# Last attention of a small vision tower: the mask multiply moves to GpSimd, one more group is scaled by ScalarE, and GpSimd's folding is cut in three

## The chip, the cores and the metric

The kernel runs on one core of a Trainium2 chip. The metric is the device time of one execution in microseconds; the time of a version is the median of its runs. Engines are called PE (TensorE), DVE (VectorE), ACT (ScalarE), POOL (GpSimd) and SP (SyncE) as in the profile.

## The reference

The program is a whole tower: 16 images of 36 tokens of 192 features go through a token embedding and four layers, each an attention-like block and a feed-forward block with residual additions. Only the attention of the last layer (L3) is touched:

```
q, k, v = split((layernorm(h) @ W_qkv + b_qkv), 12 heads of 16)
w = einsum('bhqd,bhkd->bhqk', q, k) * 16 ** -0.5       # 16 x 12 x 36 x 36
kth = top_k(w, int(0.4 * 36) = 14)[0][..., -1:]
w = where(w >= kth, w, min_val)
attn = softmax(w)
h = h + einsum('bhqk,bhkd->bqhd', attn, v).reshape(16, 36, 192) @ W_proj + b_proj
```

The feed-forward block behind it is a mixture of 16 experts with a layer norm (gain `ln_w`) ahead of each expert's second matrix. The gain can be multiplied into that matrix beforehand; this "folding" is done during the attention.

## The kernel before

The stage `layer3_attention` starts with a layer norm and the projections, then `head_attention` works on the scores. They lie as 108 rows (3 heads x 36 queries) by 64 columns of 36 keys: `sc` is `[108, 64, 36]`, a view of `padded`, whose rows are 64 apart. The 64 are cut into four groups (`BATCHES = 4`) of `CH = 16`, so one group is 108 x 576 numbers. There is no scheduler: each engine runs its own list in the order written, and semaphores join the lists.

For group g the work goes around the engines:

- PE makes the scores; ACT (`scores`, L677) copies them out of PSUM.
- DVE, `lower(g)`: top 8 of each row (L748, 16 instructions), replace them (L751, 16), top 8 of the rest (L754, 16), the maximum into `mx` (L757 or L759), and the mask `kept = (sc >= 14th)` (L760). For a group that is not `early` it then subtracts the maximum (L768).
- ACT, `exponentials(g)`: for an early group 16 instructions of 36 columns with the maximum as bias (L684), else one of 576 columns (L687). They raise `exps`.
- DVE, `normalize(g)`: multiply by `kept` (L775), sum (L776), reciprocal (L778 or L780). For an early group this raises `inverted` and ACT scales, 16 instructions of 36 columns (`scale`, L694, raising `act_probs`); else DVE scales (L781, raising `probs`).
- PE, `turn(g)` (L637): transposes the probabilities; it waits for `act_probs` or `probs`. ACT, `take_turned(g)`: first `scale(g)`, then two copies out of PSUM (L702). PE, `apply(g)` (L654): times v. ACT, `add_bias(g)` (L707).

Before, groups 0 and 1 are early (`early = BATCHES - 2`). DVE's list is lower(0), lower(1), normalize(0), lower(2), normalize(1), lower(3), normalize(2), normalize(3). ACT's list behind the scores is exponentials(0), (1), take_turned(0), exponentials(2), take_turned(1), a small copy (`keep_shifts`, L845), add_bias(0), exponentials(3), take_turned(2), add_bias(1), take_turned(3), add_bias(2), (3). PE's is `multiply` of experts 0 to 8 (L830), turn(0), `multiply` of experts 9 to 15, turn(1), apply(0), turn(2), apply(1), turn(3), apply(2), apply(3), and then the output projection (L3348).

`SecondWeights.fold` on POOL multiplies the second matrix of experts 1 to 15 by its gain, one instruction of 128 x 576 each (L840), in one loop; each waits for PE's `multiply` of the same expert. POOL does nothing else while the scores are worked on but one memset (L604).

The same `head_attention` serves the attention of layer L1 with `sparse=False` and without `also`; there `early` is 0.

Of the kernel before, what the change touches and what calls it, by code (L numbers as in the profile page):

```python
# [17 lines left out]
ALU = mybir.AluOpType  # L18
# [85 lines left out]
class Tower:  # L104
# [42 lines left out]
    def sem(self, name):  # L147

        s = self.nc.alloc_semaphore(name)
        self.of_layer.append(s)  # L150
        return s
# [409 lines left out]
def head_attention(T, ctx, block, name, ready, qk, wide, v, vb, att, sparse, also=None, space=None):  # L561
# [6 lines left out]
    BATCHES = 4  # L568
    PER = IMAGES // BATCHES
    CH = 4 * PER  # L570
# [11 lines left out]
    mx = sb("mx", [ROWS, NG])  # L582
    total = sb("total", [ROWS, NG])
    pt = sb("pt", [128, IMAGES, 2, H3, SEQ]) if space is None else space[1]
    early = BATCHES - 2 if sparse else 0
    inverted, act_probs = sem("inverted"), sem("act_probs")
    scored, sc_in, lowered, exps, probs, turned, cleared, pt_in, pv, att_in, step = map(
        sem, ("scored", "sc_in", "lowered", "exps", "probs", "turned", "cleared", "pt_in", "pv", "att_in",
              "dve_step"))
# [11 lines left out]
    @block.gpsimd  # L601
    def _(pool):
        ready(pool, True)
        pool.memset(padded[:, :, SEQ:TALL], 0.0).then_inc(cleared, 1)  # L604

    @block.tensor
    def _(pe):
# [129 lines left out]
    def _(dve):  # L737
        link = chained(dve, step)

        def lower(g):  # L740
            dve.wait_ge(sc_in, 2 * (g + 1))
            n = range(CH * g, CH * g + CH)
            part = sc[:, CH * g:CH * g + CH, :]
            top = mx[:, CH * g:CH * g + CH]
            if sparse:

                for i in n:
                    ins = dve.max(top8[:, i, :], sc[:, i, :])  # L748
                link(ins)
                for i in n:  # L750
                    ins = dve.match_replace(kept[:, i, :], top8[:, i, :], sc[:, i, :], -3.0e38)  # L751
                link(ins)
                for i in n:
                    ins = dve.max(next8[:, i, :], kept[:, i, :])  # L754
                link(ins)
                if g < early:
                    link(dve.tensor_scalar(top, top8[:, CH * g:CH * g + CH, 0], -1.0, None, ALU.mult))  # L757
                else:
                    link(dve.tensor_copy(top, top8[:, CH * g:CH * g + CH, 0]))  # L759
                link(dve.tensor_tensor(kept[:, CH * g:CH * g + CH, :], part,  # L760
                                       next8[:, CH * g:CH * g + CH, KEEP - 9:KEEP - 8].broadcast_to([ROWS, CH, SEQ]),
                                       ALU.is_ge))
            else:
                link(dve.tensor_reduce(top, part, AX.X, ALU.max))
            if g < early:
                dve.sem_inc(lowered, 1)
            else:
                dve.tensor_tensor(part, part, spread(top, 2, SEQ), ALU.subtract).then_inc(lowered, 1)  # L768

        def normalize(g):  # L770
            dve.wait_ge(exps, g + 1)
            part = sc[:, CH * g:CH * g + CH, :]
            tot = total[:, CH * g:CH * g + CH]
            if sparse:
                link(dve.tensor_tensor(part, part, kept[:, CH * g:CH * g + CH, :], ALU.mult))  # L775
            link(dve.tensor_reduce(tot, part, AX.X, ALU.add))  # L776
            if g < early:
# [4 lines left out]

        lower(0)
        lower(1)
        normalize(0)
        lower(2)
        normalize(1)
        lower(3)
        normalize(2)
        normalize(3)  # L790
# [6 lines left out]
class SecondWeights:  # L797
# [33 lines left out]
                               start=(e == 0 and f == 0), stop=(e == self.E - 1 and f == self.C - 1))  # L831
            mm.then_inc(self.summed, 1)

    def fold(self, pool):

        for e in range(1, self.E):
            w = cols(self.w[:, e, 0:self.C * DIM], self.C)
            gain = self.w[:, e, self.C * DIM:self.C * DIM + self.C]
            pool.wait_ge(self.summed, e + 1)
            pool.tensor_tensor(w, w, spread(gain, 2, DIM), ALU.mult).then_inc(self.folded, 1)  # L840
        pool.wait_ge(self.folded, self.E - 1)

    def keep_shifts(self, act, bank):
        act.wait_ge(self.summed, self.E)
# [2473 lines left out]
def layer3_attention(T):  # L3318

    nc, p = T.nc, T.p  # L3320
    with ExitStack() as ctx:
# [10 lines left out]
        att_in = head_attention(T, ctx, block, "a3_att", ready, qk, wide, v, p["avb"], att, True, second)  # L3332
        proj = cols(p["aproj"], 2)

        @block.gpsimd
        def _(pool):
            second.fold(pool)

        def at(s):
            return slice(HALF * s, HALF * s + HALF)  # L3340

# [244 lines left out]
```

## Time and profile before

| | |
|---|---|
| median of 3 runs | 841.12 us (840.67 to 842.9) |
| profiled execution | 844.89 us |
| its span in the trace | 843.0 us |
| PE busy | 749.0 us (89%) |
| DVE busy | 378.4 us (45%) |
| ACT busy | 306.2 us (36%) |
| POOL busy | 273.4 us (32%) |
| scores made to output projection of this stage | about 661 to 714 us of the span |

The profiled execution is 3.8 us above the median of the runs; a change inside it is read from its own rows and carried to the median as a difference. Times in a timeline count from the span's start. Busy shares over the whole span say little on this stage: it has 53 us of 843, and in it DVE is busy nearly throughout and PE has gaps.

### The profile page before, as it was taken

The numbers are of one execution on the slowest core, as the hardware profiler recorded it, in microseconds if no ns is written. First come the engines' busy times: TensorE is split into PE (matmuls) and PEld (weight loads), VectorE is DVE, ScalarE is ACT, GpSimd is POOL, SyncE is SP. The second block draws the span as 40 slices with busy tenths as digits, with TensorE's granted clock in tenths as the row PEclk, the third lists the DMA queues.
The fourth block names the chain that finished last, engine by engine and source line by source line (L and its number), as shares of the span: only waits on it lengthen the run. The fifth ranks groups of instructions, "written<-read, shape, count | busy, mean of one in ns | idle before, by whom it ended". The sixth has DMA issues, their size and how long they took to land. (4 is left out here: it accounts for less than half of the span.)

```text
span 843.0 us, 15814 instructions
## 1 busy us (share of the span) xinstructions
PE 749.0 (89%) x5369; PEld 558.3 (66%) x5369; DVE 378.4 (45%) x1111; ACT 306.2 (36%) x723; POOL 273.4 (32%) x316
## 2 busy tenths in 40 slices
PE   8996999798999988999977899997898967989885
PEld 5774888465585657999744788873455656666663
DVE  1354222234263257788595122221153695645543
ACT  2530222223464047666331122222234453524440
POOL 0004455100002116676023544443301161045770
PEclk9997999998989999999999999999999889879995
DMA  9815889400000052220041879626554030811224
GB/s 355 337 32 166 275 276 289 144 1 1 1 3 1 0 215 70 70 75 14 1 148 31 296 240 391 194 55 207 195 126 160 29 99 3 315 41 53 69 73 98
DMA packets 39254, 108.50 MB, mean 129 GB/s; under 512 B 5616, under 2 KB 12736, under 8 KB 38672
## 3 DMA queue, kind: packets, MB, share of 16 engines
q1 hardware_dynamic: 31584, 88.35, 30.7%
q0 software_dynamic: 7600, 19.25, 8.6%
q8 instruction: 40, 0.66, 0.3%
q14 instruction: 30, 0.25, 0.1%
HBM read 95.88 MB, written 11.70 MB: 128 GB/s over the span
## 5 line engine op out<-in xcount | busy, mean ns | idle before, releaser
L1431 POOL TENSOR_TENSOR ssm_w_low<-ssm_wbc,ssm_w_high 128x512 fp32r<-128x512 f32 x24 | 31.1, 1300 | 38.5 <-ACT ssm_w_high L1386 38.5
L157 ACT ACT_TABLE_LOAD x19 | 24.4, 1283 | 49.1 <-PEq L162 48.9
L2056 POOL TENSOR_TENSOR L_s_up<-L_s_hid,L_s_up 116x288 f32<-116x288 f32 (+1 forms) x10 | 8.3, 828 | 103.6 <-ACT L_s_up L2050 103.6
L1836 DVE TENSOR_TENSOR L_act_many<-L_hid,bank 116x384 f32<-116x384 f32 x28 | 15.5, 554 | 57.0 <-ACT L_hid L1716 44.8
L1346 PE MATMUL bank<-ssm_x_high,ssm_w_high 128*128 128x288 f32 x96 | 33.8, 352 | 3.8 <-DVE bank L1474 2.3
L1441 POOL TENSOR_TENSOR ssm_grown<-ssm_less,xn 128x576 f32<-128x576 f32 x23 | 32.9, 1430 | 8.0 <-ACT ssm_less L1414 5.3
L1691 POOL DMA_INDIRECT y_rows_L<-L_many_y,L_many_rows_out x21 | 20.7, 988 | 44.4 <-ACT L_many_y L1734 37.1
L1716 ACT ACTIVATE L_hid<-bank 116x384 f32<-116x384 f32 x28 | 13.7, 490 | 56.8 <-PE bank L1767 38.4
L1480 DVE TENSOR_TENSOR_SCAN ssm_state<-ssm_decay,bank 128x576 f32<-128x576 f32 x24 | 32.5, 1354 | 0.8
L2025 PE MATMUL bank<-xn,par_L1f 128*116 128x288 f32 (+1 forms) x128 | 31.0, 455 | 0.1
L1666 POOL DMA_INDIRECT L_many_xr<-x_rows_L,L_many_rows_in x27 | 26.8, 994 | 11.9 <-issue 10.6
L2981 DVE TENSOR_TENSOR L_act<-L_hid,bank 128x384 f32<-128x384 f32 x18 | 10.0, 554 | 45.1 <-ACT L_hid L2950 32.4
L1346 PE MATMUL bank<-ssm_x_low,ssm_w_high 128*128 128x288 f32 x96 | 28.8, 300 | 0.0
L1346 PE MATMUL bank<-ssm_x_high,ssm_w_low 128*128 128x288 f32 x96 | 28.7, 299 | 0.0
L1346 PE MATMUL bank<-ssm_x_mixed,ssm_w_high 128*128 128x288 f32 x96 | 28.6, 298 | 0.0
L1346 PE MATMUL bank<-ssm_x_top,ssm_w_low 128*128 128x288 f32 x96 | 28.5, 297 | 0.0
L1356 PE MATMUL bank<-ssm_out,ssm_sum_w 128*128 128x288 f32 x96 | 27.3, 406 | 0.0
L2950 ACT ACTIVATE L_hid<-bank 128x384 f32<-128x384 f32 x18 | 8.8, 489 | 50.5 <-PE bank L2920 50.5
L2868 POOL DMA_INDIRECT y_rows_L<-L_yb,L_rows_out x18 | 17.8, 989 | 24.9 <-ACT L_yb L2956 21.6
L297 PE MATMUL bank<-h,par_const 128*128 128x288 f32 x64 | 19.1, 446 | 7.4 <-PEq L162 7.4
L3077 PE MATMUL bank<-L_w,L_xtb 128*128 x68 | 24.8, 486 | 0.0
L1762 PE MATMUL bank<-L_many_xt,L_w 128*116 128x192 f32 x128 | 24.6, 335 | 0.0
(550 smaller groups left out, 1938.4 us busy)
## 6 DMA issues: line engine op xcount, KB each, us to landing
L_w<-in_L2w SPq DMA_DIRECT2D x14, 696.0 KB, 7.1
L_more<-in_L2w SPq DMA_DIRECT2D x10, 696.0 KB
L_w<-in_L0w SPq DMA_DIRECT2D x12, 576.0 KB
ssm_wbc<-in_wBC SPq DMA_DIRECT2D x24, 256.0 KB
L_w<-in_L3w SPq DMA_DIRECT2D x5, 1152.0 KB
L_w<-in_L2w SPq DMA_DIRECT2D x14, 384.0 KB
L_more<-in_L0w SPq DMA_DIRECT2D x9, 576.0 KB
second<-in_L3w SPq DMA_DIRECT2D x16, 291.0 KB
```

The source lines that it names most:

```text
L157: self.nc.scalar.activation(self.unread[:, at:at + 1], self.p["ones"][:, 0:1], func)
L297: mm = pe.matmul(T.bank[s][:, 0:HALF], mean[:, c, :], self.x[:, c, HALF * s:HALF * s + HALF], start=(c == 0), stop=(c == 1))
L1346: mm = pe.matmul(T.bank[2 * a + s][:, 0:HALF], w[t % NW][:, at:at + 128], x[:, HALF * s:HALF * s + HALF], start=(n == 0), stop=(n == len(t ...
L1356: mm = pe.matmul(T.bank[2 * SUM_AT + s][:, 0:HALF], sum_w[t % NB][:, :], out[t % NB][:, HALF * s:HALF * s + HALF], start=t in (0, REST_TILES),
L1431: pool.tensor_tensor(w_low[t % NW][:, :], wbc[t % NW][:, :], w_high[t % NW][:, :], ALU.subtract).then_inc(low, 1)
L1441: pool.tensor_tensor(grown[t % NB][:, :], less[t % NB][:, :], xs[:, of(t), :], ALU.mult).then_inc(grown_made, 1)
L1480: dve.tensor_tensor_scan(st[:, :], d[:, :], drive, 0.0, ALU.mult, ALU.add).then_inc(scanned, 1)
L1666: pool.indirect_dma_start(self.xr[j][:, :], None, self.X.x_rows[:, :], bass.IndirectOffsetOnAxis(ap=self.rows_in[h][:, u:u + 1], axis=0))\
L1691: pool.indirect_dma_start(X.y_rows[:, :], bass.IndirectOffsetOnAxis(ap=self.rows_out[h][:, u:u + 1], axis=0), self.y[U * h + u][:, :], Non ...
L1762: pe.matmul(bank[0:N, MANY * f:MANY * f + MANY], w1[:, at:at + N], self.xt[h][:, 0, rows], start=(f == 0), stop=False)
L2025: mm = pe.matmul(self.T.bank[bank + u % self.RING][0:self.N, 0:HALF], self.w1[lanes, c, at:at + self.N], self.T.xn[lanes, c, HALF * s:HALF ...
L3077: mm = pe.matmul(self.up_bank[u % 2][:, 0:I], self.X.xt[u % 4][:, c, :], self.w1[:, bass.ds(e * (2 * I) + (I * c - 2 * I), I)], start=(c = ...
```

## The change

Three edits, all in the sparse case of `head_attention`:

1. `early` goes from 2 to 3: group 2 gets its exponentials in 16 ACT instructions with a bias, no subtraction on DVE, and is scaled by ACT in 16 instructions and not by DVE.
2. For the three early groups POOL multiplies `sc` by `kept` (new L609) once ACT has raised `exps`, and raises `masked`; DVE's `normalize` waits for that and only sums and inverts. Group 3 is multiplied by DVE as before.
3. The folding goes into POOL's list in parts: experts 1 to 4 behind the multiply of group 0, 5 to 8 behind that of group 1, 9 to 15 behind that of group 2. On DVE, normalize(0) and (1) move behind the first 16 instructions of lower(2) and lower(3).

```diff
--- before.py
+++ after.py
@@ -582,8 +582,8 @@
     mx = sb("mx", [ROWS, NG])
     total = sb("total", [ROWS, NG])
     pt = sb("pt", [128, IMAGES, 2, H3, SEQ]) if space is None else space[1]
-    early = BATCHES - 2 if sparse else 0
-    inverted, act_probs = sem("inverted"), sem("act_probs")
+    early = BATCHES - 1 if sparse else 0
+    inverted, act_probs, masked = map(sem, ("inverted", "act_probs", "masked"))
     scored, sc_in, lowered, exps, probs, turned, cleared, pt_in, pv, att_in, step = map(
         sem, ("scored", "sc_in", "lowered", "exps", "probs", "turned", "cleared", "pt_in", "pv", "att_in",
               "dve_step"))
@@ -602,6 +602,13 @@
     def _(pool):
         ready(pool, True)
         pool.memset(padded[:, :, SEQ:TALL], 0.0).then_inc(cleared, 1)
+        if also:
+            for g in range(early):
+                at = slice(CH * g, CH * g + CH)
+                pool.wait_ge(exps, g + 1)
+                pool.tensor_tensor(sc[:, at, :], sc[:, at, :], kept[:, at, :], ALU.mult).then_inc(masked, 1)
+                also.fold(pool, 4 * g + 1, min(4 * g + 5, also.E) if g < early - 1 else also.E)
+            pool.wait_ge(also.folded, also.E - 1)
 
     @block.tensor
     def _(pe):
@@ -747,6 +754,8 @@
                 for i in n:
                     ins = dve.max(top8[:, i, :], sc[:, i, :])
                 link(ins)
+                if g >= 2:
+                    normalize(g - 2)
                 for i in n:
                     ins = dve.match_replace(kept[:, i, :], top8[:, i, :], sc[:, i, :], -3.0e38)
                 link(ins)
@@ -768,10 +777,13 @@
                 dve.tensor_tensor(part, part, spread(top, 2, SEQ), ALU.subtract).then_inc(lowered, 1)
 
         def normalize(g):
-            dve.wait_ge(exps, g + 1)
             part = sc[:, CH * g:CH * g + CH, :]
             tot = total[:, CH * g:CH * g + CH]
-            if sparse:
+            if g < early:
+                dve.wait_ge(masked, g + 1)
+            else:
+                dve.wait_ge(exps, g + 1)
+            if sparse and g >= early:
                 link(dve.tensor_tensor(part, part, kept[:, CH * g:CH * g + CH, :], ALU.mult))
             link(dve.tensor_reduce(tot, part, AX.X, ALU.add))
             if g < early:
@@ -782,9 +794,11 @@
 
         lower(0)
         lower(1)
-        normalize(0)
+        if not sparse:
+            normalize(0)
         lower(2)
-        normalize(1)
+        if not sparse:
+            normalize(1)
         lower(3)
         normalize(2)
         normalize(3)
@@ -831,14 +845,13 @@
                                start=(e == 0 and f == 0), stop=(e == self.E - 1 and f == self.C - 1))
             mm.then_inc(self.summed, 1)
 
-    def fold(self, pool):
-
-        for e in range(1, self.E):
+    def fold(self, pool, first, end):
+
+        for e in range(first, end):
             w = cols(self.w[:, e, 0:self.C * DIM], self.C)
             gain = self.w[:, e, self.C * DIM:self.C * DIM + self.C]
             pool.wait_ge(self.summed, e + 1)
             pool.tensor_tensor(w, w, spread(gain, 2, DIM), ALU.mult).then_inc(self.folded, 1)
-        pool.wait_ge(self.folded, self.E - 1)
 
     def keep_shifts(self, act, bank):
         act.wait_ge(self.summed, self.E)
@@ -3332,10 +3345,6 @@
         att_in = head_attention(T, ctx, block, "a3_att", ready, qk, wide, v, p["avb"], att, True, second)
         proj = cols(p["aproj"], 2)
 
-        @block.gpsimd
-        def _(pool):
-            second.fold(pool)
-
         def at(s):
             return slice(HALF * s, HALF * s + HALF)
 
```

DVE's list, from the last two instructions of lower(1), twelve rows. `a_att_sc` are the scores, `a_att_kept` the mask, `a_att_top`, `a_att_next` the top values, `a_att_mx` the maxima, `a_att_total` the sums. Before:

```order
L757 TENSOR_SCALAR a_att_mx<-a_att_top 108x16
L760 TENSOR_TENSOR a_att_kept<-a_att_sc,a_att_next 108x576
L775 TENSOR_TENSOR a_att_sc<-a_att_sc,a_att_kept 108x16x36
L776 TENSOR_REDUCE a_att_total<-a_att_sc 108x16
L778 RECIPROCAL a_att_total<-a_att_total 108x16
L748 MAX a_att_top<-a_att_sc 108x8 x16
L751 MATCH_REPLACE a_att_kept<-a_att_top,a_att_sc 108x36 x16
L754 MAX a_att_next<-a_att_kept 108x8 x16
L759 COPY a_att_mx<-a_att_top 108x16
L760 TENSOR_TENSOR a_att_kept<-a_att_sc,a_att_next 108x576
L768 TENSOR_TENSOR a_att_sc<-a_att_sc,a_att_mx 108x16x36
L775 TENSOR_TENSOR a_att_sc<-a_att_sc,a_att_kept 108x16x36
```

And in the changed kernel, from the same place:

```order
L766 TENSOR_SCALAR a_att_mx<-a_att_top 108x16
L769 TENSOR_TENSOR a_att_kept<-a_att_sc,a_att_next 108x576
L755 MAX a_att_top<-a_att_sc 108x8 x16
L788 TENSOR_REDUCE a_att_total<-a_att_sc 108x16
L790 RECIPROCAL a_att_total<-a_att_total 108x16
L760 MATCH_REPLACE a_att_kept<-a_att_top,a_att_sc 108x36 x16
L763 MAX a_att_next<-a_att_kept 108x8 x16
L766 TENSOR_SCALAR a_att_mx<-a_att_top 108x16
L769 TENSOR_TENSOR a_att_kept<-a_att_sc,a_att_next 108x576
L755 MAX a_att_top<-a_att_sc 108x8 x16
L788 TENSOR_REDUCE a_att_total<-a_att_sc 108x16
L790 RECIPROCAL a_att_total<-a_att_total 108x16
```

The multiply by the mask (L775) has left the list; the sum and the reciprocal stand between the first and the second kind of instruction of the next group; group 2 has a TENSOR_SCALAR for its maximum (L766) and no subtraction.

ACT's list from the scaling of group 0 to the copies of group 2. Before:

```order
L694 ACTIVATE a_att_sc<-a_att_sc,a_att_total 108x36 x16
L702 COPY a_att_pt<-bank 128x432 x2
L687 ACTIVATE a_att_sc<-a_att_sc 108x16x36
L694 ACTIVATE a_att_sc<-a_att_sc,a_att_total 108x36 x16
L702 COPY a_att_pt<-bank 128x432 x2
L845 ACTIVATE sw_shift<-bank 16x192
L707 ACTIVATE a_att<-bank,par_L3a 96x144 x2
L687 ACTIVATE a_att_sc<-a_att_sc 108x16x36
L702 COPY a_att_pt<-bank 128x432 x2
```

And in the changed kernel (L701 is the scaling, L691 and L694 the two kinds of exponential, L709 the copies):

```order
L701 ACTIVATE a_att_sc<-a_att_sc,a_att_total 108x36 x16
L709 COPY a_att_pt<-bank 128x432 x2
L691 ACTIVATE a_att_sc<-a_att_sc,a_att_mx 108x36 x16
L701 ACTIVATE a_att_sc<-a_att_sc,a_att_total 108x36 x16
L709 COPY a_att_pt<-bank 128x432 x2
L858 ACTIVATE sw_shift<-bank 16x192
L714 ACTIVATE a_att<-bank,par_L3a 96x144 x2
L694 ACTIVATE a_att_sc<-a_att_sc 108x16x36
L701 ACTIVATE a_att_sc<-a_att_sc,a_att_total 108x36 x16
```

Group 2's one exponential is now 16, and 16 instructions of scaling stand ahead of its copies.

POOL's list behind its memset was one row before, fifteen times L840. In the changed kernel it is (L609 the multiply by the mask, L854 the folding):

```order
L609 TENSOR_TENSOR a_att_sc<-a_att_sc,a_att_kept 108x16x36
L854 TENSOR_TENSOR second<-second 128x576 x4
L609 TENSOR_TENSOR a_att_sc<-a_att_sc,a_att_kept 108x16x36
L854 TENSOR_TENSOR second<-second 128x576 x4
L609 TENSOR_TENSOR a_att_sc<-a_att_sc,a_att_kept 108x16x36
L854 TENSOR_TENSOR second<-second 128x576 x7
```

The folding of experts 1 to 4, 5 to 8 and 9 to 15 now stands behind one multiply each.

## Rows read from the trace of the kernel before

**Rows 1.** Waits between 662 and 716 us: engine, line, released by: total, times, longest.
```profile
PE bank L637 <- ACT a_att_sc L694: 6.4, 1, 6.4
PE bank L637 <- DVE a_att_sc L781: 3.8, 1, 3.8
```

**Rows 2.** Timeline of PE: start us, us, instruction, count, idle before it.
```profile
686.50 3.20 PE L637 MATMUL bank<-par_const,a_att_sc 108*64 108x108 f32 x32 [6.43 <-ACT a_att_sc L694]
689.43 7.57 PE L830 MATMUL bank<-second,sw_cols 128*48 128x192 f32 x42
696.84 1.70 PE L637 MATMUL bank<-par_const,a_att_sc 108*64 108x108 f32 x32
...
703.00 2.12 PE L637 MATMUL bank<-par_const,a_att_sc 108*64 108x108 f32 x32 [3.80 <-DVE a_att_sc L781]
...
706.16 2.45 PE L637 MATMUL bank<-par_const,a_att_sc 108*64 108x108 f32 x32
...
709.82 4.15 PE L3348 MATMUL bank<-a_att,par_L3a 96*128 96x288 f32 x16
```

**Rows 3.** Timeline of ACT.
```profile
679.45 3.55 ACT L684 ACTIVATE a_att_sc<-a_att_sc,a_att_mx 108x36 f32<-108x36 f32 x16 [4.91 <-DVEq L766]
682.91 3.54 ACT L694 ACTIVATE a_att_sc<-a_att_sc,a_att_total 108x36 f32<-108x36 f32 x16
...
689.74 0.52 ACT L702 COPY a_att_pt<-bank 128x432 f32<-128x432 f32 x1 [0.92 <-PE bank L637]
690.15 0.69 ACT L687 ACTIVATE a_att_sc<-a_att_sc 108x576 f32<-108x576 f32 x1
691.58 3.55 ACT L694 ACTIVATE a_att_sc<-a_att_sc,a_att_total 108x36 f32<-108x36 f32 x16 [0.74 <-DVE a_att_total L778]
...
699.47 0.64 ACT L707 ACTIVATE a_att<-bank,par_L3a 96x144 f32<-96x144 f32 x2
700.44 0.68 ACT L687 ACTIVATE a_att_sc<-a_att_sc 108x576 f32<-108x576 f32 x1 [0.33 <-DVE a_att_sc L768]
```

**Rows 4.** Timeline of DVE.
```profile
671.04 1.66 DVE L748 MAX8 a_att_top<-a_att_sc 108x8 f32<-108x36 f32 x16
...
677.18 0.49 DVE L757 TENSOR_SCALAR a_att_mx<-a_att_top 108x16 f32<-108x16 f32 x1
677.71 1.66 DVE L760 TENSOR_TENSOR a_att_kept<-a_att_sc,a_att_next 108x576 f32<-108x576 f32 x1
679.51 1.47 DVE L775 TENSOR_TENSOR a_att_sc<-a_att_sc,a_att_kept 108x576 f32<-108x576 f32 x1
681.01 0.75 DVE L776 TENSOR_REDUCE a_att_total<-a_att_sc 108x16 f32<-108x576 f32 x1
681.80 0.25 DVE L778 RECIPROCAL a_att_total<-a_att_total 108x16 f32<-108x16 f32 x1
...
689.72 0.75 DVE L775 TENSOR_TENSOR a_att_sc<-a_att_sc,a_att_kept 108x576 f32<-108x576 f32 x1
...
704.72 0.76 DVE L781 TENSOR_TENSOR a_att_sc<-a_att_sc,a_att_total 108x576 f32<-108x576 f32 x1
```

**Rows 5.** Timeline of POOL in narrow stretches; the last row a whole run of folds.
```profile
677.60 1.14 POOL L840 TENSOR_TENSOR second<-second 128x576 f32<-128x576 f32 x1
678.71 1.65 POOL L840 TENSOR_TENSOR second<-second 128x576 f32<-128x576 f32 x1
...
691.22 7.78 POOL L840 TENSOR_TENSOR second<-second 128x576 f32<-128x576 f32 x7 [8.13 <-PE bank L830]
```

**Rows 6.** An earlier line of POOL: count, then ns min/median/max, first and last start.
```profile
L1441 POOL TENSOR_TENSOR ssm_grown<-ssm_less,xn x23: 1415/1428/1439, 323.4 to 399.6; 128x576 f32<-128x576 f32 x23
```

**Rows 7.** Windows: us, busy (count) of PE, PEld, DVE, ACT, POOL, clock, DMA share, GB/s.
```profile
686.40:690.00 3.60, 3.50 (x34) 3.34 (x35) 3.50 (x20) 0.83 (x3) 0.00 (x0) 0.50 0.00 0
...
697.00:700.00 3.00, 2.19 (x81) 1.94 (x77) 2.90 (x9) 1.89 (x5) 2.00 (x2) 1.00 0.00 0
...
704.20:707.60 3.40, 3.40 (x76) 3.06 (x73) 1.46 (x4) 1.53 (x4) 0.00 (x0) 0.50 0.02 5
```

## Prediction

> **What bounds the kernel now.** Only the stretch from the scores to the output projection of the last attention is edited, so I read the waits of that stretch first, then the timelines of its engines. The waits show where PE, which carries the stage to its end, stands still: 6.4 us for ACT's scaling of group 0 and 3.8 us for DVE's scaling of group 2 [rows 1]. On PE's timeline these are the gaps ahead of 686.50 and 703.00; turn(1) at 696.84 has no gap ahead of it, since the multiply of experts 9 to 15 runs until then; and from 703.00 on PE runs without a gap to the projection at 709.82 [rows 2]. So the end is set by when turn(2) starts, and what it waits for.
>
> Two chains lead there. DVE's: it works from 671.04 to 705.48 [rows 4], and its scaling of group 2 is what released turn(2) at 703.00 [rows 1, 2]. ACT's: group 1's exponentials 679.45 to 683.00, scaling of group 0 until 686.45, turn(0), its second copy until 690.26, exponential of group 2 (0.69), scaling of group 1, copies, a bias that ends at 700.11, exponential of group 3 at 700.44 [rows 3]. That last row waited only 0.33 us for DVE: ACT's chain is just behind DVE's already. The reader is to see that the two are nearly level, so that work cannot be moved from DVE to ACT for nothing.
>
> **What DVE loses.** Three multiplies by the mask, one subtraction and one scaling, all of 108 x 576 with two inputs: 0.75 us each where nothing disturbs them, 1.47 us for the one at 679.51 [rows 4]. That is 5 x 0.75 plus 0.7, about 4.4 us, and if DVE alone set turn(2) this would be the gain. Moving normalize(0) behind the first sixteen instructions of lower(2) costs nothing: ACT can't scale group 0 before its exponentials of group 1 end at 683.00, and these start when lower(1) ends.
>
> **What ACT gets.** Group 2's exponentials as sixteen take 3.55 us instead of 0.69, and its scaling is 3.55 more [rows 3]. I walk the chain with before's times. After the second copy of turn(0), ACT starts the sixteen exponentials at 690.15; they end at 693.70, the scaling of group 1 at 697.25. Turn(0) began 0.05 us after its scaling, so turn(1) begins at 697.30 instead of 696.84 (PE's multiply hid the rest). Before, ACT was free for group 3's exponential 3.27 us after turn(1) began (696.84 to 700.11); now at 700.60. It takes 0.68, then comes the new scaling, 3.55: 704.83. Turn(2) starts at 704.88 instead of 703.00: **+1.88 us**. Nothing hides it, for PE stands idle already.
>
> **What POOL gets.** Each multiply by the mask is bounded from below by a fold, 1.14 us, and from above by the undisturbed 1.44 of a multiply of 128 x 576 with two full inputs [rows 5, 6]; I take 1.43, as the kept mask too is a full input. None lies on the path: the one of group 0 starts at about 674.6 (3.55 us after the group's exponentials begin at about 671) and is wanted at 681. Then four folds at (7.78 - 1.15) / 6 = 1.11 us a step [rows 5] run until 680.4, ahead of the end of group 1's exponentials at 683.0; four more end by 689.4 and group 2's exponentials at 694. The last seven folds end near 705 instead of 699, where nothing waits for them before the block ends near 715.
>
> **What POOL does to DVE.** The fold that began at 677.60 held up the instructions at 677.18 (0.49) and, after the next small gap, at 677.71 (1.66 where 0.76 is usual), and the fold at 678.71 then took 1.65 instead of 1.14, the DVE instruction in between [rows 4, 5]: the two engines take turns, and a DVE instruction of two inputs that meets a fold loses up to about 1.1 us. The Trainium skill ("SBUF — State Buffer", section "Who interferes with whom") says that a Vector instruction with two SBUF inputs and a GpSimd one that reads SBUF exclude each other for the whole instruction, and that whichever was issued first holds the ports; this trace agrees (1.66 and 1.65 us where 0.76 and 1.14 are usual). The rule speaks against the change, since POOL gets 18 such instructions instead of 15 and spreads them over more of DVE's list: if the waits stayed as the rows of before have them, the sum below would be +1.2 us, and if each further meeting costs a wait, it is +2.2.
>
> I take two terms. First, lower(1): POOL's folds stand at 676.0, 677.1 and 678.2 now, so the maximum at 677.18 comes just behind the start of one and waits to 678.2, not 677.6; the end of lower(1), and all of ACT's chain with it, moves from 679.37 to 679.96, **+0.6**. Bounds: no meeting at all, 677.18 + 0.17 + 0.76 = 678.1, -1.2; the worst phase +0.7. Second, group 3: lower(2) took 6.14 us of its own kind from its start to the maximum (as 671.04 to 677.18 for the pass before [rows 4]); with the sum and the inverse (0.75 + 0.25) inside and two waits for folds lower(2) ends at about 690.1 and lower(3) finds its maximum at 697.3. Its last three instructions (copy, mask, subtraction) now fall into the seven folds, wait for one each, and end at about 701.2; before, POOL was done at 699.0 [rows 5] and they ended ahead of 700.44 [rows 3]. Sum and inverse of group 2 come behind them, 702.3, and ACT wants them at 701.3 + 0.6 = 701.9: **+0.4**, with 0 and +1.2 as bounds. DVE's 4.4 us are thus spent on waiting for POOL and on standing behind ACT. Group 3's probabilities, by the same rows about 706, are wanted at 708 or later.
>
> **PE's clock.** Turn(0) took 3.20 us at a granted clock of 0.50 (1.2 GHz), turn(1) 1.70 at 1.00 (2.4 GHz) [rows 2, 7]. Turn(2) to turn(3) took 2.12 and 2.45, because the clock fell to 0.50 from 704.2 to 707.6 after the idle time ahead of 703.00 [rows 2, 7]. With turn(2) at 704.88 + 0.6 + 0.4 = about 705.9, less work lies in that half-clock stretch: 1.7 us of it instead of 3.4, so half of 1.7 is regained, less a little for copies: **-0.7**, if the clock rises at the same place. If it doesn't, nothing is regained and about 0.8 more is lost.
>
> **Sum.** +1.88 + 0.6 + 0.4 - 0.7 = **+2.2 us**: the profiled execution from 844.9 to 847.1, and the median, which lies 3.8 below the profiled execution, from 841.12 to **843.3**.
>
> **Rivals.**
> - The clock stays low behind 707.6, since PE's pause ahead of turn(2) grows from 3.8 to above 5 us. Then the rest of turn(2), apply(1) and most of turn(3) run at half the clock until about 711: +1.5 on the forecast, +3.7, 844.8. For it speaks that turn(0) stayed at 0.50 after a pause of 6.4 us; against it, that 704.2 to 707.6 was followed by a rise with much the same work in it. This is the case slower by more than 0.3%; it decides if PE's start of turn(2) comes later than about 706. Chance 0.24.
> - DVE, not ACT, sets turn(2): every instruction of two inputs in lower(2) and lower(3) waits for a full fold, and the order to scale comes a microsecond and more later than I took: +3.2, 844.3, slower. Chance 0.14.
> - POOL misses DVE in lower(1) and half the half-clock loss goes too: 1.88 - 1.2 - 1.4 = -0.7, 840.4, faster but inside 0.3%. It needs the phase of POOL's folds to fall right. Chance 0.12. That more is gained needs ACT's sixteen to be quicker than its rows; 0.06 for all that.
> - The change does not do what it says: POOL reaches the multiply late, behind folds, and DVE waits for `masked`. The slack is 683.0 - 680.4 = 2.6 us at group 1 and about 4.9 at group 2; it decides only if a fold took 1.8 us or more. Chance 0.02, time 844 to 846.
>
> **How the numbers follow.** The forecast has 0.42; its own range is 841.5 to 843.9 (below, the first term at -1.2 in place of +0.6; above, the second at +1.0 in place of +0.4). A measurement of this kernel tells about 0.3%, 2.5 us, from no change, which is 843.6. Faster by that: 0.06. Slower: both slower rivals, 0.38, and a part of the forecast's upper edge beside a part of these two that stays below, 0.38 in all. Same: 0.56. The range for 8 in 10 is 841.2 to 845.2: from the lower end of the forecast's own to the clock rival with its spread.
>
> **What would show each step.** Right: ACT without a gap from turn(0)'s second copy to turn(1), two runs of 3.55 us; PE's wait ahead of turn(2) released by ACT's scaling and 5 to 6 us long; DVE's list shorter in instructions but ending after 704; DVE's mask instructions at 1.2 to 1.7 us in all four groups; POOL's multiplies at 1.4 us. Wrong: turn(2) released before 703, or released by DVE; mask instructions at 0.76 us; a multiply on POOL well over 2 us; the clock at 0.50 after 707.6.

## The result and the profile after

The changed kernel takes 847.65 us in the median (843.14 to 853.73, 9 runs), the kernel before beside it 841.71; the ratio is 1.0095, interval 1.0064 to 1.0126. It is slower: by 5.9 us as the medians stand, by 8 us (5.4 to 10.6) as the ratio does, where 2.2 were predicted. (Ratios here and below are of undisturbed executions and need not equal the quotient of two medians.) The profiled execution has a span of 849.7 us, 6.7 more than before's.

Executions differ by several us ahead of this stage, so I compare the **stretch** from DVE's first MAX8 of the stage to PE's first instruction of the output projection: 663.79 to 709.82 before [rows 2], **46.0 us**, and 665.50 to 719.23 after, **53.7 us**. The 7.7 us of difference are as large as the whole loss, so it arises here.

The waits of the changed kernel between 664 and 726 us (engine and line, released by: total, times, longest):

```profile
PE bank L644 <- ACT a_att_sc L701: 17.1, 2, 8.9
...
ACT a_att_sc L694 <- DVE a_att_sc L777: 3.5, 1, 3.5
```

PE's second pause grew from 3.8 to 8.9 us. It is released by ACT and no longer by DVE [rows 1], as predicted, though 5 to 6 us of it were expected; but ACT itself waits 3.5 us for DVE's subtraction of group 3, where it waited 0.33 [rows 3]. PE's timeline after, answering to [rows 2]:

```profile
689.93 3.20 PE L644 MATMUL bank<-par_const,a_att_sc 108*64 108x108 f32 x32 [8.15 <-ACT a_att_sc L701]
692.86 8.35 PE L844 MATMUL bank<-second,sw_cols 128*48 128x192 f32 x42
701.05 1.70 PE L644 MATMUL bank<-par_const,a_att_sc 108*64 108x108 f32 x32
...
712.34 3.20 PE L644 MATMUL bank<-par_const,a_att_sc 108*64 108x108 f32 x32 [8.94 <-ACT a_att_sc L701]
...
716.37 1.75 PE L644 MATMUL bank<-par_const,a_att_sc 108*64 108x108 f32 x32
...
719.23 4.15 PE L3357 MATMUL bank<-a_att,par_L3a 96*128 96x288 f32 x16
```

ACT's, answering to [rows 3]:

```profile
682.87 3.55 ACT L691 ACTIVATE a_att_sc<-a_att_sc,a_att_mx 108x36 f32<-108x36 f32 x16 [6.62 <-DVEq L775]
...
693.58 3.55 ACT L691 ACTIVATE a_att_sc<-a_att_sc,a_att_mx 108x36 f32<-108x36 f32 x16
697.03 3.54 ACT L701 ACTIVATE a_att_sc<-a_att_sc,a_att_total 108x36 f32<-108x36 f32 x16
...
703.68 0.64 ACT L714 ACTIVATE a_att<-bank,par_L3a 96x144 f32<-96x144 f32 x2
707.78 0.68 ACT L694 ACTIVATE a_att_sc<-a_att_sc 108x576 f32<-108x576 f32 x1 [3.46 <-DVE a_att_sc L777]
708.74 3.55 ACT L701 ACTIVATE a_att_sc<-a_att_sc,a_att_total 108x36 f32<-108x36 f32 x16 [0.27 <-DVE a_att_total L790]
```

And what DVE did meanwhile, answering to [rows 4]: of groups 1, 2 and 3 the instruction that writes 16 maxima, and the comparison behind it.

```profile
678.89 2.20 DVE L766 TENSOR_SCALAR a_att_mx<-a_att_top 108x16 f32<-108x16 f32 x1
681.13 1.65 DVE L769 TENSOR_TENSOR a_att_kept<-a_att_sc,a_att_next 108x576 f32<-108x576 f32 x1
...
689.96 1.29 DVE L766 TENSOR_SCALAR a_att_mx<-a_att_top 108x16 f32<-108x16 f32 x1
691.28 1.65 DVE L769 TENSOR_TENSOR a_att_kept<-a_att_sc,a_att_next 108x576 f32<-108x576 f32 x1
...
700.12 5.16 DVE L768 COPY a_att_mx<-a_att_top 108x16 f32<-108x16 f32 x1
705.31 1.65 DVE L769 TENSOR_TENSOR a_att_kept<-a_att_sc,a_att_next 108x576 f32<-108x576 f32 x1
706.99 0.76 DVE L777 TENSOR_TENSOR a_att_sc<-a_att_sc,a_att_mx 108x576 f32<-108x576 f32 x1
```

A copy of 16 elements a partition took 5.16 us. It takes 0.17 where nothing is in its way. POOL's timeline shows what was:

```profile
676.33 1.40 POOL L609 TENSOR_TENSOR a_att_sc<-a_att_sc,a_att_kept 108x576 f32<-108x576 f32 x1 [10.52 <-ACT a_att_sc L691]
677.71 4.45 POOL L854 TENSOR_TENSOR second<-second 128x576 f32<-128x576 f32 x4
686.50 1.40 POOL L609 TENSOR_TENSOR a_att_sc<-a_att_sc,a_att_kept 108x576 f32<-108x576 f32 x1 [4.34 <-ACT a_att_sc L691]
687.87 4.45 POOL L854 TENSOR_TENSOR second<-second 128x576 f32<-128x576 f32 x4
697.21 1.41 POOL L609 TENSOR_TENSOR a_att_sc<-a_att_sc,a_att_kept 108x576 f32<-108x576 f32 x1 [4.89 <-ACT a_att_sc L691]
698.57 7.78 POOL L854 TENSOR_TENSOR second<-second 128x576 f32<-128x576 f32 x7
```

The reader is to see the seven folds of the last row: 1.11 us apart, the COPY arrives at 700.12, in the second of them (699.68 to 700.8), and ends at 705.28, just as the last one begins at 705.20. Folds took 1.15 us each in that time, so POOL lost nothing; DVE waited through five of them, the one that ran and four that were let in ahead of it. In groups 1 and 2 the same instruction was passed over by one fold in a run of four, and the comparison behind it waited for the last fold.

Where the 7.7 us arise, as differences of the two timelines: first MAX8 to ACT's exponentials of group 1 (they start when lower(1) ends), 15.66 to 17.37, +1.7; turn(0) to turn(1), +0.8; turn(1) to the exponential of group 3, 3.60 to 6.73, +3.1; from there to turn(2), 2.56 to 4.56, +2.0; turn(2) to the projection, 6.82 to 6.89, +0.1.

The +0.8 is not ACT's. Its scaling of group 1 ended at 700.57, but PE's multiply ran until turn(1) at 701.05: it took 8.35 us, 7.57 before [rows 2], at a lower granted clock. The window of that multiply, columns as in [rows 7], before and after:

```profile
689.50:696.80 7.30, 7.30 (x45) 5.41 (x42) 7.16 (x62) 4.65 (x18) 5.58 (x6) 0.93 0.01 3
692.90:701.00 8.10, 8.10 (x45) 5.83 (x42) 7.82 (x68) 7.41 (x33) 3.79 (x4) 0.83 0.01 3
```

### The profile page after: what moved, and what is told of

Read it like the earlier page. It is cut to its first block and busy times, and to the rows that moved or that the text cites. A ratio compares the mean times of both kernels' runs of the same rounds, so it can differ in the third digit from the quotient of the medians.

```text
span 849.7 us, 15846 instructions
## 1 busy us (share of the span) xinstructions
PE 756.6 (89%) x5369; PEld 564.0 (66%) x5369; DVE 382.4 (45%) x1106; ACT 313.3 (37%) x754; POOL 275.9 (32%) x319
## 5 line engine op out<-in xcount | busy, mean ns | idle before, releaser
L157 ACT ACT_TABLE_LOAD x19 | 24.4, 1283 | 49.1 <-PEq L162 48.9
L2038 PEld LDWEIGHTS bank<-xn,par_L1f 128*116 128x116 f32 (+1 forms) x128 | 16.2, 193 | 14.8 <-issue 12.9
```

Of the source, the lines that this page charges most:

```text
L157: self.nc.scalar.activation(self.unread[:, at:at + 1], self.p["ones"][:, 0:1], func)
L2038: mm = pe.matmul(self.T.bank[bank + u % self.RING][0:self.N, 0:HALF], self.w1[lanes, c, at:at + self.N], self.T.xn[lanes, c, HALF * s:HALF ...
```

## The experiments

Twelve further kernels in sixteen experiments, four of which repeat an earlier one. The stretch is read from one profile each; the ratio is to the kernel before, run beside it. A `...` in an excerpt stands for lines left out.

| kernel | stretch, us | ratio | interval |
|---|---|---|---|
| before | 46.0 | | |
| changed | 53.7 | 1.0095 | 1.0064 to 1.0126 |
| reduce_max | 53.0 | 1.0074 | 1.0034 to 1.0113 |
| folds_late | 46.6 | 0.9978 | 0.9942 to 1.0015 |
| act_two | 49.3 | 1.0056 | 1.0012 to 1.01 |
| act_three_only | 49.6 | 0.9982 | 0.9946 to 1.0017 |
| placed (first) | 42.5 | 0.9978 | 0.995 to 1.0007 |
| before_no_folds | 41.9 | 0.9956 | 0.9921 to 0.9992 |
| spacer | 53.9 | 1.0086 | 1.0044 to 1.0128 |
| fold_thirds | 46.7 | 0.9985 | 0.9955 to 1.0014 |
| before_thirds | 44.2 | 0.9983 | 0.9952 to 1.0013 |
| act_two_thirds | 49.1 | 1.0013 | 0.9981 to 1.0045 |
| fold_two_parts | 48.3 | one run | |
| placed_again | 42.9 | 0.9966 | 0.9932 to 1.0 |
| after_again | 53.7 | one run | |
| act_two_thirds_again | 42.3 | one run | |
| before_placed | 41.8 | 0.995 | 0.992 to 0.9981 |
| placed_third | 42.9 | 0.995 | 0.9914 to 0.9985 |

### reduce_max: the small instruction in another form

```diff
-                    link(dve.tensor_scalar(top, top8[:, CH * g:CH * g + CH, 0], -1.0, None, ALU.mult))
+                    link(dve.tensor_reduce(top, top8[:, CH * g:CH * g + CH, 0:1], AX.X, ALU.max, negate=True))
                 else:
-                    link(dve.tensor_copy(top, top8[:, CH * g:CH * g + CH, 0]))
+                    link(dve.tensor_reduce(top, top8[:, CH * g:CH * g + CH, 0:1], AX.X, ALU.max))
```

> All times run from DVE's first MAX8 of the stage to PE's first instruction of the output projection: 46.0 us before, 53.7 after. Edit: in the changed kernel the small instruction that writes the row maxima (TENSOR_SCALAR for groups 0 to 2, COPY for group 3, 108 x 16) becomes a TENSOR_REDUCE of the same 16 elements. Theory (that small instruction can't get in between GpSimd's back-to-back folds and waits until the last one of a run; a reduction does not need what GpSimd holds): the reductions take 0.1 to 0.3 us where 2.20, 1.29 and 5.16 us stood, DVE is no longer late for group 3's exponential, and the stretch falls to 47.5 to 49.5 us. Rival 1 (every DVE instruction in that place waits for the folds): the reductions take 2 to 5 us and the stretch stays at 53 to 54. Rival 2 (ACT's sixteen and sixteen are the loss): the waits may go, but the stretch stays above 52.

The reductions took 0.18 us each. But the stretch stayed at 53.0 us, since the wait went to the next instruction; DVE's timeline of this kernel in group 3:

```profile
693.40 0.18 DVE L768 TENSOR_REDUCE a_att_mx<-a_att_top 108x16 f32<-108x16 f32 x1
693.62 6.63 DVE L769 TENSOR_TENSOR a_att_kept<-a_att_sc,a_att_next 108x576 f32<-108x576 f32 x1
```

Half of my theory fell here, and the range of 47.5 to 49.5 us with it. A reduction is not held up by folds, but it isn't the small instructions that are special: a TENSOR_TENSOR of two SBUF inputs is kept out as long, 5.87 us. The Trainium skill ("SBUF — State Buffer", "Who interferes with whom") has the same split: a copy and a tensor_scalar can contend with GpSimd, an instruction with two SBUF inputs does when GpSimd reads SBUF, and a reduction never does on Trainium2.

### folds_late: masks on GpSimd, folds behind everything

```diff
-                also.fold(pool, 4 * g + 1, min(4 * g + 5, also.E) if g < early - 1 else also.E)
+            pool.wait_ge(lowered, BATCHES)
+            also.fold(pool, 1, also.E)
```

> Edit: in the changed kernel GpSimd multiplies by the mask as written, but folds all fifteen experts only after DVE has finished lowering group 3. Theory: the small instructions take 0.17 us, the mask comparisons 0.76, the stretch from DVE's first MAX8 to the output projection is 46.5 to 48.5 us, and DVE's multiply and scaling of group 3 meet the folds instead, off the path; the fifteen folds (16.6 us) may end after PE's projection and give back 0 to 2 us at the end of the block. Rival (the third scaling group on ACT and the half clock are the loss): above 51 us.

46.6 us, in the expected range. The maxima of groups 1 and 2 took 0.17 us and all comparisons 0.76; the COPY of group 3 met the end of a mask multiply (0.54). The fifteen folds ended 2.9 us behind the start of the projection, and the next block began 52.6 us behind the first MAX8 (52.0 before). So with the folds out of DVE's way the changed kernel is level with the one before. That doesn't make masks on GpSimd and a third group on ACT free, for the kernel before has waits for folds in its 46.0 us as well (before_no_folds and before_placed, below, have 41.9 and 41.8). What holds this kernel at 46.6 is ACT. PE's timeline of it:

```profile
705.74 3.20 PE L645 MATMUL bank<-par_const,a_att_sc 108*64 108x108 f32 x32 [4.98 <-ACT a_att_sc L702]
```

### act_two: ACT as before

```diff
-    early = BATCHES - 1 if sparse else 0
+    early = BATCHES - 2 if sparse else 0
+    on_pool = BATCHES - 1 if sparse else 0
...
-            for g in range(early):
+            for g in range(on_pool):
...
```

> Edit: in the changed kernel only groups 0 and 1 are scaled by ACT, as before; group 2 is subtracted and scaled by DVE and gets one exponential, but GpSimd still multiplies three groups by the mask and folds in three parts. Theory (folds hold up DVE's small instructions): the small instruction of group 3 still takes 3 us or more, and the stretch from DVE's first MAX8 to the output projection is 49.5 to 52 us, of 53.7: ACT's part is worth 2 to 4 us. Rival (ACT's third group is the loss): the stretch returns to 46 to 47.5.

49.3 us, a little below the range and 4.4 below the changed kernel. Not all of it is ACT's third group: the COPY of group 3 took 3.02 us, 2.1 less than there. It came later in the run of seven folds, and was passed over to the very end of it.

### act_three_only: one number changed in the kernel before

```diff
-    early = BATCHES - 2 if sparse else 0
+    early = BATCHES - 1 if sparse else 0
```

> Edit: in the kernel before, only the number of groups scaled by ACT goes from 2 to 3; masks on DVE, folds in one loop. Theory: the small instructions take at most 0.5 us as before, turn(2) starts about 1.9 us later, the stretch from DVE's first MAX8 to the output projection is 46.8 to 48.5 us (46.0 before). Rival (ACT's third group is the loss of the change): 51 us or more.

49.6 us, between theory and rival. PE's timeline of this kernel:

```profile
706.99 3.20 PE L637 MATMUL bank<-par_const,a_att_sc 108*64 108x108 f32 x32 [6.19 <-ACT a_att_sc L694]
```

From its first MAX8 at 664.98 turn(2) starts 42.0 us later, 39.2 before: +2.8. Of this 1.06 is ACT waiting for DVE to invert group 2, on ACT's timeline,

```profile
703.38 3.55 ACT L694 ACTIVATE a_att_sc<-a_att_sc,a_att_total 108x36 f32<-108x36 f32 x16 [1.06 <-DVE a_att_total L778]
```

and 1.74 is the rest of ACT's chain, where I summed +1.88. Another 0.7 us is PE's clock: all of turn(2) runs at 0.50 here. The whole run does not show these 3.5 us (0.4%): its ratio is 0.9982, with an interval that ends at 1.0017. Why the profile and the runs disagree here is open.

### placed: a version made from the readings

ACT scales two groups (`early` back to 2), GpSimd multiplies three (`on_pool` is 3).

```diff
...
+            for g in range(on_pool):
+                at = slice(CH * g, CH * g + CH)
+                if g:
+                    pool.wait_ge(lowered, g + 1)
+                    also.fold(pool, 4 * g - 3, 4 * g + 1)
+                pool.wait_ge(exps, g + 1)
+                pool.tensor_tensor(sc[:, at, :], sc[:, at, :], kept[:, at, :], ALU.mult).then_inc(masked, 1)
+            pool.wait_ge(probs, BATCHES - early)
+            also.fold(pool, 9, also.E)
...
```

> Edit: GpSimd multiplies three groups by the mask as in the changed kernel, ACT scales only two as before, and the folds stand where DVE runs only instructions that do not meet them: experts 1 to 4 once lower(1) is done, 5 to 8 once lower(2) is done, 9 to 15 once DVE has finished its last scaling. Theory (the loss is DVE held up by folds; the masks on GpSimd are a gain by themselves): the small instructions take 0.17 us and the comparisons 0.76, from DVE's first MAX8 to the output projection 41 to 43.5 us (46.0 before, 53.7 after), the run 3 to 5 us below before. Rival (GpSimd's multiplies themselves hold DVE up, or ACT is the bound): 45 us or more, no faster than before.

No DVE instruction waited for POOL, and the stretch was 42.5 us, 3.6 below before. The run itself gave 0.9978 with an interval up to 1.0007, so it was repeated twice, below. 3 to 5 us less were expected of the run, and that did not come.

### before_no_folds: what folds cost before

```diff
-        @block.gpsimd
-        def _(pool):
-            second.fold(pool)
```

> Edit: the kernel before without the folds on GpSimd (the gain is not multiplied into experts 1 to 15, work left out). It measures what folds cost already before. Theory: the comparisons of groups 1 and 3 and the mask of group 0 lose their waits (0.3 + 0.9 + 0.7 and 0.2 + 0.9 us), of which 2 to 3 us lie on the path: from DVE's first MAX8 to the output projection 43 to 44.5 us. Rival (waits were hidden behind ACT and PE): 45.5 to 46.

The folds are left out, so the layer norm gain is missing from experts 1 to 15. 41.9 us, more than expected: DVE's waits of 3.05 us in total, and the half clock that PE had in turn(2) and turn(3) is gone too (each 1.75 us; 2.12 and 2.45 in [rows 2]).

### spacer: a gap between folds

```diff
             pool.tensor_tensor(w, w, spread(gain, 2, DIM), ALU.mult).then_inc(self.folded, 1)
+            pool.memset(self.spare[:, e:e + 1], 0.0)
```

> Edit: in the changed kernel each fold is followed by a memset of one column on GpSimd, an instruction that reads nothing. Theory (DVE cannot get in between folds because one follows the other at once; one wait is several folds long): with a gap after each fold DVE gets in after at most one fold, the COPY of group 3 waits at most 1.2 us instead of 4.99, and the stretch from DVE's first MAX8 to the output projection falls from 53.7 to 49 to 51 us. Rival (GpSimd keeps DVE out until its queue is nearly empty, whatever stands in it): the COPY waits 5 us or more, 53 us or more.

(The excerpt leaves out the line that allots `spare`.) The expectation failed and the rival's numbers came: the COPY took 5.23 us, the stretch 53.9. A memset of one column between folds, itself 0.09 to 0.13 us and laid over the fold's end, lets DVE in no sooner.

### fold_thirds: short folds

```diff
-            pool.tensor_tensor(w, w, spread(gain, 2, DIM), ALU.mult).then_inc(self.folded, 1)
+            for c in range(self.C):
+                ins = pool.tensor_tensor(w[:, c:c + 1, :], w[:, c:c + 1, :], spread(gain[:, c:c + 1], 2, DIM), ALU.mult)
+            ins.then_inc(self.folded, 1)
```

> Edit: in the changed kernel each fold is three instructions of 128 x 192 instead of one of 128 x 576. If DVE gets in only near the end of a run of back-to-back instructions, its longest wait stays at 4 to 7 us, and the stretch from DVE's first MAX8 to the output projection is 53 us or more; if it loses a fixed small number of turns, the waits fall to a third, below 2 us, and the stretch to 48 to 50.5 us.

46.7 us, below both expected ranges: every DVE instruction waited at most 0.25 us. The changed kernel with this one edit is level with before. DVE's and POOL's timelines of group 3:

```profile
696.90 0.20 DVE L768 COPY a_att_mx<-a_att_top 108x16 f32<-108x16 f32 x1
697.13 1.00 DVE L769 TENSOR_TENSOR a_att_kept<-a_att_sc,a_att_next 108x576 f32<-108x576 f32 x1
698.17 0.94 DVE L777 TENSOR_TENSOR a_att_sc<-a_att_sc,a_att_mx 108x576 f32<-108x576 f32 x1
```

```profile
696.97 11.89 POOL L855 TENSOR_TENSOR second<-second 128x192 f32<-128x192 f32 x21
```

I took this for a rule (short instructions let DVE in) and tried it in three more places.

### before_thirds, act_two_thirds, fold_two_parts, placed_again

> Edit: the kernel before with each fold as three instructions of 128 x 192. Theory (DVE loses time to folds before too, and short folds let it in at each turn): waits of DVE's instructions of at most 0.3 us each; from DVE's first MAX8 to the output projection 42.5 to 44 us (46.03 before, 41.94 without folds), the run 2 to 4 us below before. Rival (that stretch was short without folds for another reason, the clock of PE for one): 45 us or more.

44.2 us (0.2 above the range), longest wait 0.31 us; the run 0.9983, not told apart from before (2 to 4 us less were expected).

> Edit: the changed kernel with ACT scaling two groups only and each fold as three instructions; masks of three groups on GpSimd, folds behind them as in the changed kernel. Theory: DVE has three multiplies less and short waits: 41.5 to 43.5 us from DVE's first MAX8 to the output projection, as for the version with placed folds (42.48), the run 3 to 6 us below before. Rival (moving the masks to GpSimd is worth nothing): the same as the kernel before with folds in thirds, or above it.

49.1 us, and this is what broke the rule: groups 1 and 2 lost at most 0.25 us a time, but the COPY of group 3 was passed over by all the short folds up to the end of the run.

```profile
693.25 6.42 DVE L769 COPY a_att_mx<-a_att_top 108x16 f32<-108x16 f32 x1
```

> Edit: in the changed kernel each fold is two instructions, 128 x 384 and 128 x 192. If the length of the instruction that holds the ports decides whether DVE gets its turn (576 columns: no, 192: yes), DVE gets in behind a 192 part and often not behind a 384 part: waits of at most 1.5 us, 47 to 49 us from DVE's first MAX8 to the projection. If the number of instructions in a row decided it, the waits would be as long as with one instruction or with three.

(With `w[:, 0:2]` and `w[:, 2:3]` as the two parts.) 48.3 us, longest wait 0.75 us, so shorter than with one instruction; that fits the expectation but, after the run beside it, doesn't show that length decides.

> The same text as the version with placed folds, run beside the others: 42 to 43 us from DVE's first MAX8 to the projection again, and 2 to 6 us below before if its first result (0.9978, interval 0.995 to 1.0007) is a gain and not chance; within 1 us of the masks-on-GpSimd version with folds in thirds.

42.9 us again.

### after_again, act_two_thirds_again, before_placed, placed_third

These were run to see whether the long waits repeat, and what of the placed version is due to the masks.

> The changed kernel once more. If the long waits belong to the places in the program, the three small instructions take 2.2, 1.3 and 5.2 us again within 0.1 us and the stretch from DVE's first MAX8 to the output projection is 53 to 54.5 us; if they are chance, at least one differs by a whole fold (1.1 us).

They repeat: 2.20, 1.29 and 5.15 us in an execution whose stage began 4.7 us earlier, the stretch 53.7 again. DVE's timeline of the repeat:

```profile
674.24 2.20 DVE L766 TENSOR_SCALAR a_att_mx<-a_att_top 108x16 f32<-108x16 f32 x1
...
695.47 5.15 DVE L768 COPY a_att_mx<-a_att_top 108x16 f32<-108x16 f32 x1
```

> ACT scaling two groups, masks on GpSimd, folds in thirds, once more. If the wait of 6.25 us of group 3's COPY belongs to the place, it comes again and the stretch is 49 us; if it is chance, the COPY waits below 0.5 us and the stretch is 42 to 44 us.

Here it did not: the COPY took 0.40 us and the stretch was 42.3 us.

```profile
699.29 0.40 DVE L769 COPY a_att_mx<-a_att_top 108x16 f32<-108x16 f32 x1
```

The COPY came 0.16 us behind the start of a short fold in the first execution and 0.14 us in this one. So one and the same kernel, at nearly the same phase, gives 6.25 us of waiting or 0.23; whether the 0.02 us decide or something that the profile doesn't show is not known. The spread of the 12 runs of act_two_thirds, 838.9 to 849.98 us, says nothing on how often it turns over: the kernel before spread at least as widely beside them.

> Edit: the kernel before with only the folds placed (experts 1 to 5 once DVE has inverted group 0's sums, 6 to 9 once it has inverted group 1's, 10 to 15 once its last scaling is done), masks on DVE. Theory (all of the gain is from placing, the masks on GpSimd are worth nothing, since ACT and PE's multiply hold the end as well): no DVE instruction waits, 42 to 43.2 us from DVE's first MAX8 to the output projection, the ratio to before within 0.3% of the placed version's. Rival (taking three masks off DVE is a gain by itself): 1 us or more above the placed version's 42.5 to 42.9.

```diff
...
+            pool.wait_ge(inverted, 1)
+            also.fold(pool, 1, 6)
+            pool.wait_ge(inverted, 2)
+            also.fold(pool, 6, 10)
+            pool.wait_ge(probs, BATCHES - early)
+            also.fold(pool, 10, also.E)
...
```

(The excerpt leaves out that the loop over all experts behind the stage is gone and `fold` takes its bounds.) 41.8 us with the masks left on DVE, 0.2 below the range; the rival would have had 43.5 or more. Ratio 0.995, interval 0.992 to 0.9981: this is the simplest version that beats both kernels. PE's timeline of it:

```profile
697.32 1.70 PE L645 MATMUL bank<-par_const,a_att_sc 108*64 108x108 f32 x32
...
701.09 1.75 PE L645 MATMUL bank<-par_const,a_att_sc 108*64 108x108 f32 x32 [1.41 <-DVE a_att_sc L789]
...
703.88 1.75 PE L645 MATMUL bank<-par_const,a_att_sc 108*64 108x108 f32 x32 [0.39 <-DVE a_att_sc L789]
```

> The version with masks on GpSimd and placed folds beside it: 42 to 43 us, ratio to before 0.994 to 0.999.

42.9 us and 0.995, interval 0.9914 to 0.9985: level with before_placed.

### What the experiments say together

Two parts of the change cost time. Each is read as a difference of stretches, from one profile a kernel.

- **The folds in DVE's way** cost 4.2 us in the kernel before (46.0 against 41.8 with the folds placed) and 7.1 in the changed one (53.7 against 46.6 in folds_late). So the new places add 2.9 us.
- **A third group on ACT and the masks on GpSimd** cost 4.8 us where no fold is in the way (46.6 against 41.8): 3.4 up to turn(2) and 1.3 behind it, where turn(2) takes 3.20 us and not 1.75. Nearly all is the third group: folds_late against the three runs of placed, which differ in it and in where the folds stand, gives 3.7 to 4.1 us, and act_three_only against before 3.5.

Together that is the 7.7. The whole runs confirm the first part (1.0095 against 0.9978, intervals apart) and are too coarse for the second (0.9978 against 0.995, intervals overlapping). The two can't be told apart on the timelines of before and after alone: there DVE's waits for folds hide a part of ACT's longer list.

## Why the prediction was wrong

- **Which stretch, and that turn(2) sets its end:** right. PE's pause ahead of turn(2) is released by ACT's scaling and everything behind follows at the same distance (6.8 and 6.9 us).
- **ACT's third group, +1.88:** right in mechanism, and in size as a step from the kernel before. From the start of group 3's exponential to turn(2) I had 0.68 + 3.55 + 0.05 = 4.28 us; it was 4.56, with 0.27 of waiting for the inverse. act_three_only has 1.74 for this chain. With the waits in lower(1) gone, my walk gives 46.0 + 1.88 - 1.2 = 46.7 us, and folds_late has 46.6. The part of it that turn(1) was to bring, +0.46, was +0.8, and came from PE's multiply at a lower clock. What I didn't see is that the same waits hold up DVE in the kernel before: without them DVE lets turn(2) start 36.2 us behind the first MAX8 (before_placed), where ACT's longer list lets it start after 39.6 (folds_late).
- **"the maximum at 677.18 comes just behind the start of one and waits to 678.2", +0.6:** this is the step that failed first. The phase was right (it came 0.07 us behind a fold's start; that the fold of 677.60 held up the instruction of 677.18 in the kernel before was a misreading, it was the one ahead of it, and the sum did not use it), but it was let in not behind that fold but behind the next: lower(1) ended 1.7 us late, outside the bound of +0.7 that I had drawn from one meeting costing at most one fold.
- **"Its last three instructions ... wait for one each", +0.4:** the step that cost most. The COPY alone waited 4.99 us. ACT stood 3.46 us, where my upper bound was 1.2. In [rows 4] and [rows 5] DVE got in after one fold every time, and I made a law of it. folds_late and fold_thirds, which leave the rest of the change as it is, take 7.1 and 7.0 us off the stretch. (The end of the last seven folds, "near 705", was also off: 694 + 1.43 + 7.78 is 703.2.)
- **The forecast in the pieces of the result:** +0.6, +0.5, -0.3, +2.1 and -0.7, where +1.7, +0.8, +3.1, +2.0 and +0.1 were measured. Of the 5.5 us that it missed, 4.5 are the two places at which DVE waited for more than one fold, and 0.8 the clock of PE behind turn(2).
- **The clock, -0.7:** wrong. Turn(2) ran in full at half the clock (3.20 us), turn(3) at the full one (1.75). What one gained the other lost. The windows of the changed kernel, columns as in [rows 7]:

```profile
712.30:715.50 3.20, 3.16 (x35) 2.90 (x36) 0.00 (x0) 0.52 (x1) 0.00 (x0) 0.50 0.02 5
715.90:719.20 3.30, 3.30 (x167) 3.10 (x159) 0.00 (x0) 2.25 (x7) 0.00 (x0) 0.97 0.00 0
```

- **The rivals:** the right one was DVE setting turn(2) (chance 0.14), but priced at one fold a meeting, +3.2. POOL's multiplies took 1.40 us (1.43 assumed) and were never late, so the fourth rival was rightly small.
- **DVE's 4.4 us:** the changed kernel realises none, as forecast, and no version tried has them either: with the folds placed, three masks on GpSimd (42.5 to 42.9 us) are no better than masks on DVE (41.8), and with the subtraction and the scaling on ACT too it is 46.6 (folds_late).

What stays open is what decides whether DVE is let in at the next fold. Not the length of the fold alone (act_two_thirds), not a small gap between folds (spacer), not the kind of DVE instruction among those that contend (reduce_max). It repeated at equal phases in one kernel (after_again) and turned over at phases 0.02 us apart in another (act_two_thirds and its repeat), and I found no rule in the phase that holds for all cases. That all of a run's folds are ready to go is not enough either: in folds_late they were, and DVE's scaling of group 3, which came 0.14 us behind the start of the sixth of fifteen, got in at the seventh. The rule of the Trainium skill that the prediction cites, that whichever was issued first holds the ports, doesn't carry over to the next instruction: in the changed kernel four folds that started after the COPY had come went ahead of it.

## What to carry to other kernels

While GpSimd runs back-to-back instructions that read SBUF, price a DVE copy, tensor_scalar or two-input instruction not at one GpSimd instruction of waiting but at anything up to the rest of the run, and don't take a trace in which it got in after one as the rule. Start such a run by a semaphore that DVE raises when it turns to instructions that don't contend (MAX8, MATCH_REPLACE8, reductions), and make it no longer than they last; here that was worth 0.5% (interval 0.2 to 0.8%), and what GpSimd took over from DVE was worth nothing. Before calling a change level with the kernel before, give the kernel before the same cure: folds_late looked free beside 46.0 us and is 4.8 us worse than before_placed. Before moving work off the engine that released the last wait, look at how far behind the next chain is: it was 0.33 us.

## What the runs showed of the hardware

- A COPY of 108 x 16 waited through five GpSimd instructions of 1.15 us in a row (4.99 us), through fourteen of 0.5 us in another kernel (6.25 us), and a TENSOR_TENSOR with two SBUF inputs through six of 1.15 us (5.87 us), while GpSimd's own instructions kept their undisturbed times.
- Where DVE was passed over by 576-column folds, it came in just ahead of the last fold of the run in the changed kernel, reduce_max, spacer and groups 1 and 2 of act_two, and only behind it in group 3 of act_two.
- MAX8, MATCH_REPLACE8, RECIPROCAL and TENSOR_REDUCE kept their times beside folds in all kernels (a TENSOR_REDUCE of 108 x 16: 0.18 us in the place where the COPY took 5.16).
